# A GpSimd clear of 1024 columns behind each group of four gathers or scatters, in a graph network on one core

## The reference

```python
edge_index = jnp.stack([src, dst])
x = _layernorm(x + _L0_gnn_ref(x, edge_index, ...))                # two GCN layers
x = _layernorm(x + _L1_gnn_ref(x, edge_index, edge_attr_16, ...))  # gated messages, batch norm, layer norm
x = _layernorm(x + _L2_gnn_ref(x, edge_index, edge_attr_16, ...))  # attention with three heads
x = _layernorm(x + _L3_gnn_ref(x, edge_index, batch0, ...))        # six GCN layers, 128-64-32-16-32-64-128
return x

def _gcn_conv(h, W, b, row, col, norm, num_nodes):
    h = h @ W
    msg = h[row] * norm[:, None]
    agg = jax.ops.segment_sum(msg, col, num_segments=num_nodes)
    return agg + b
# gated block: z = concat(x[dst], x[src], edge_attr); msg = sigmoid(z @ Wf.T + bf) * softplus(z @ Ws.T + bs); segment_sum over dst
```

## Time and profile before

| | |
|---|---|
| median of three runs | 11513.55 us (11469.03 to 11515.87) |
| the profiled execution, own time | 11609.91 us |
| its span, first to last instruction | 11608.2 us |
| mean granted TensorE clock | 0.676 of full |
| busy: PE, DVE, ACT, POOL | 57%, 69%, 51%, 64% of the span |
| passes by the span's time | first 0-690, g1 690-1453, g2 1453-2395, gated edges 2395-3562, gated nodes 3562-4751, two attention passes 4751-5701 and 5701-6969, g3 6969-7683, g4 7683-8303, g5 8303-9053, g6 9053-9694, g7 9694-10335, g8 10335-11608 |

### The profile page before, as it was taken

How to read it: one execution, slowest core, us unless ns; L and a number is a source line. 1 busy time by engine, 2 the same in 40 slices (tenths; PEclk the granted TensorE clock), 3 DMA queues, 4 the chain that set the end, 5 groups by cost and what they waited for, 6 DMA issues and landing times. The chain is left out here.

```text
span 11608.2 us, 141508 instructions
## 1 busy us (share of the span) xinstructions
PE 6579.4 (57%) x32436; PEld 5426.1 (47%) x32436; DVE 8028.9 (69%) x33105; ACT 5915.6 (51%) x13869; POOL 7392.5 (64%) x6801
## 2 busy tenths in 40 slices
PE   6036666656664666677656665754455565643343
PEld 3035556645554666677646665642233343422222
DVE  7347799956667999899888884445466666764444
ACT  0024467757667999898667772321133232322222
POOL 7734478867776888666467764556545555556666
PEclk8568888878886555688778885555577555655555
DMA  4977678832224777444345553433344333322221
GB/s 137 302 241 237 235 268 290 289 114 71 71 70 139 236 234 236 144 141 140 107 139 176 176 172 107 136 102 83 85 128 132 89 98 88 120 85 55 56 58 54
DMA packets 1019495, 1694.44 MB, mean 146 GB/s; under 512 B 304877, under 2 KB 535080, under 8 KB 1018594
## 3 DMA queue, kind: packets, MB, share of 16 engines
q1 hardware_dynamic: 782752, 1361.06, 35.0%
q0 software_dynamic: 175936, 218.82, 8.4%
q10 hardware_dynamic: 59970, 105.49, 2.7%
HBM read 988.03 MB, written 707.78 MB: 146 GB/s over the span
## 5 line engine op out<-in xcount | busy, mean ns | idle before, releaser
L1340 POOL DMA_INDIRECT g_got<-scaled,row_src x2352 | 2230.9, 949 | 1651.4 <-issue 679.7
L298 PE MATMUL g_a_p_z<-sb_L_gnn_W,g_a_u_t 128*128 128x128 f32 (+3 forms) x2574 | 653.1, 398 | 1046.4 <-ACT g_a_u_t L1185 375.4
L902 DVE SCALAR_TENSOR_TENSOR g_sums<-g_got,first,g_sums 128x128 f32<-128x128 f32 (+3 forms) x3136 | 869.1, 277 | 395.0 <-issue 111.4
L298 PEld LDWEIGHTS g_a_p_z<-sb_L_gnn_W,g_a_u_t 128*128 128x128 f32 (+1 forms) x2574 | 483.6, 266 | 1219.5 <-issue 562.4
L906 DVE SCALAR_TENSOR_TENSOR g_sums<-g_sums,cont,g_got 128x128 f32<-128x128 f32 (+3 forms) x3128 | 884.7, 283 | 121.6 <-DVE g_sums L902 91.9
L1185 ACT COPY g_a_u_t<-g_a_p_t 128x512 f32<-128x512 f32 (+3 forms) x495 | 225.3, 455 | 1350.4 <-remote 735.5
L298 PE MATMUL g_bb_p_z<-sb_L_gnn_W,g_bb_u_t 128*128 128x128 f32 (+2 forms) x4302 | 836.2, 362 | 121.8 <-DVE g_bb_z L1077 78.6
L298 PEld LDWEIGHTS g_bb_p_z<-sb_L_gnn_W,g_bb_u_t 128*128 128x128 f32 x4302 | 755.8, 262 | 170.9 <-issue 141.7
L1185 ACT COPY g_bb_u_t<-g_bb_p_t 128x1024 f32<-128x1024 f32 (+2 forms) x294 | 233.8, 795 | 1143.2 <-PE g_bb_p_t L289 591.1
L1340 POOL DMA_INDIRECT g_got<-xs,idx_src x392 | 370.8, 946 | 481.4 <-DVE g_a_own L1021 271.3
L1252 POOL DMA_INDIRECT out<-g_a_o,idx_out x396 | 395.3, 998 | 351.6 <-ACT g_a_o L350 222.3
(11 more groups left out here) (495 smaller groups left out, 23743.0 us busy)
## 6 DMA issues: line engine op xcount, KB each, us to landing
raw<-gb_u SPq DMA_DIRECT2D x98, 768.0 KB
xs<-f_o ACTq DMA_DIRECT2D x97, 516.0 KB
f_x<-in_x ACTq DMA_DIRECT2D x97, 512.0 KB
g_bb_own<-in_x SPq DMA_DIRECT2D x97, 512.0 KB
wide<-g_bb_o SPq DMA_DIRECT2D x97, 512.0 KB
g_bb_own<-wide SPq DMA_DIRECT2D x97, 512.0 KB
g_bb_res<-in_x SPq DMA_DIRECT2D x97, 512.0 KB
x<-g_bb_o SPq DMA_DIRECT2D x97, 512.0 KB
```

Of the source, the lines that this page charges most:

```text
L298: last = nc.tensor.matmul(dst_psum[0:p, q * g * width:(q * g + n) * width], turned_tile[0:n * k, q * P:q * P + p], weight[0:n * k, 0:n * w ...
L902: nc.vector.scalar_tensor_tensor(out=self.firsts, in0=new, scalar=first[:, col], in1=self.firsts, op0=ALU.mult, op1=ALU.add).then_inc(run_ ...
L1340: pool.indirect_dma_start(got[b.s4][:, c * row:(c + 1) * row], None, table, bass.IndirectOffsetOnAxis(ap=index[:, b.n * CH + c:b.n * CH + ...
```

## The change

A tile `idle` of 128 partitions by 1024 columns is added to the graph passes and to the gated edge pass. GpSimd clears it behind each block's four gathers in g1 and g3 to g8, behind each block's four scatters in g8, and in the gated edge pass twice a block, behind the four gathers of source rows and behind the four of destination rows. Before each clear it waits for the semaphore increment of the clear before. Nobody reads the tile. g2 is left as it is, as are the passes that are not of these two kinds. That is 98 clears in each of g1 and g3 to g7, 197 in g8 and 196 in the gated edge pass, 981 in all. No other engine's instructions change.

```diff
+REST = 1024
@@ graph_pass
+                idle = sb("idle", [P, REST])
                     def _(pool):
+                        rests = Steps(pool_step, 999)
+
+                        def rest(b):
+
+                            if rests.k:
+                                pool.wait_ge(pool_step, rests.k)
+                            nc.gpsimd.memset(idle[:, :], 0.0).then_inc(pool_step, 1)
+                            rests.count()
+
                         if scatters:
-                            pipeline(pool, [(gather, 0, NBE), (na.scatter, 4, NBA)])
+                            pipeline(pool, [(gather, 0, NBE), (rest, 0, NBE), (na.scatter, 4, NBA), (rest, 4, NBA)])
                             na.scatters_done()
                         elif normal:
...
                         else:
-                            pipeline(pool, [(gather, 0, NBE)])
+                            pipeline(pool, [(gather, 0, NBE), (rest, 0, NBE)])
```

## The result

The changed kernel takes 11157.92 us (median of 4 runs, 11127.33 to 11172.85), the kernel before beside it 11508.53 us (4 runs). The ratio is 0.970, 95% interval 0.968 to 0.972. I had said 11245 us: right in sign, 87 us too high. The profiled execution took 11144.9 us with a span of 11142.8, 465 us less than before. Of these 465 us only 351 are the change: the profiled execution of the kernel before took 11609.91 us, 101 us above its median, and that of the changed kernel 13 us less than its own.

What follows compares the result with a forecast made beforehand. Waits bound the touched passes, as signals are held during GpSimd's descriptor making. Waits -974 and clears +657 give -317; with the gated pass +74 less some 25, about -270: 11610 to 11340, scaled to 11245 us; range 11120 to 11420.

Steps and rivals of the forecast that it cites:

- What bounds the kernel: Touched passes: waits set their length; signals are held while GpSimd makes descriptors; GpSimd's waits in graph passes total 1299 us.
- Cost of a clear: GpSimd's list: a clear takes 0.98 us and adds 0.84 us, 824 us in all.
- The wait for the clear before: Before each clear: taken as 0, at most 1226 us if its signal is held.
- How many of the waits go: Seven graph passes: three quarters of GpSimd's 1299 us of waits go, -974 us; with added clears, -317 us.
- hand-over: Time a held signal needs to pass when GpSimd pauses: 1.25 us after four gathers, 2.4 after 12.
- GpSimd's floor: Each pass's length minus GpSimd's waits plus added clears; the seven graph passes go from 5402 to 4760 us.
- The gated pass: Gated pass: 165 us of clears added, 91 us of waits gone; +74 us, less some 25 for released signals.
- The cover: GpSimd's waits hide the clears; if the waits stay, the clears come on top.
- A: Touched passes: the pause cures everything, every pass at its floor, -568 us, total 10950 us; chance 0.13.
- B: End of the clear: the pause is too short, holds last longer, kernel slower at 11860 us; chance 0.25.
- C: Waits absorb the clears and no more: 650 us go against 657 added, some 11530 us; chance 0.14.
- The rule on ports: g1 and gated pass: a clear could block a two-port VectorE copy; at most 192 us, left out of the sum.

Runs made afterwards that it cites:

- e4: Changed kernel with each of the 981 clears replaced by GpSimd waiting until its four indirect DMAs have landed; 12013.6 us, ratio 1.046 to the kernel before.
- e6: Changed kernel with a clear of 256 columns behind each indirect DMA instead of 1024 behind each four; ratio 0.972 to the kernel before.
- e1: Changed kernel with its 981 clears 16 columns wide instead of 1024; ratio 1.000 to the kernel before.
- e5: Changed kernel without the 196 clears of the gated pass, graph passes as changed; 11085 us, ratio 0.965 to the kernel before.
- e9: Changed kernel with a clear of 128 columns behind each indirect DMA instead of 1024 behind each four; 11428 us, ratio 0.985 to the kernel before.
- e2: Changed kernel with its clears 512 columns wide instead of 1024; ratio 0.984 to the kernel before.
- e7: Changed kernel with one clear of 2048 columns behind each eight indirect DMAs instead of 1024 behind each four; ratio 0.980 to the kernel before.
- e11: On e5, g1 with 256 columns behind each gather, g4 with 512 columns, g8 with 768; 11123 us, ratio 0.959 to the kernel before.
- e10: Graph passes alone, one clear of 4096 columns behind each sixteen indirect DMAs instead of 1024 behind four; 11580 us, ratio 0.998 to the kernel before.

## Why the prediction was right, and where its sizes were off

**What bounds the kernel.** Right: what held the engines was GpSimd's stream of indirect DMAs. Spreading that stream, with nothing else changed, removes the remote waits of g3 to g8 (e4) or of g8 and the gated pass (e6), and adding instructions without time (e1) does not.

**Cost of a clear.** 0.98 us forecast, 0.97 measured; 0.16 us to the next indirect DMA, as forecast; 0.84 us on the list. In g5 GpSimd's busy time grew by 95 us and its 98 shorter gaps gave 14 back, 81 against 82.

**The wait for the clear before.** Taken as 0, measured 0.4 us in all 981.

**How many of the waits go.** This step was mis-sized, by less than the two profiles say. I took three quarters of 1299 us, 974. Between the two profiles 1130 went, and the graph passes became 497 us shorter against a forecast of 317. But the profile before is of an execution 101 us above the median. The kernel with clears of 16 columns (e1, ratio 1.000) has a profile of 11507.6 us, 1 us from that median. Its seven graph passes add up to 5300 us, and its GpSimd waits 1198 us for buffers and scatter rows. Against it the changed kernel's passes are 407 us shorter and some 1030 us of the waits are gone, 86%. So the graph passes brought 90 us more than forecast, and the gated pass cost 14 more; with what the other stretches and the executions differ by, that makes the 87 us by which I was too high. Of the 90 us, 55 are waits; the rest I cannot assign.

Behind it stands a wrong reason: I set the pause of 1.14 us against a hand-over of 1.25 us and called it slightly too short, as if the hand-over were a fixed time. It grows with the run. e6 has pauses of 0.5 us and does nearly as well, so what four leave behind is not a threshold to be met. That the time came out near is in part luck: three quarters was a guess between all and none.

g6 and g7 end at GpSimd's floor (582 and 584 us against a forecast floor of 581 each), g4 at 592 under its floor of 602, g8 at 1183 under 1216. The stretches of the earlier trace rows had made g4's and g8's floors 10 and 20 us too long, and g1's 25 us too short.

**The gated pass.** +49 forecast, +55 measured between the two profiles (+63 against e1's), and e5 takes it away. The floor was the right account: GpSimd waited there for 91 us of remote releases and 20 us of TensorE, these 111 us went, and the clears added 165, which makes +54. The cover was smaller than the cost from the start, as the prediction's own 91 against 165 said; the edit could have been left out there.

**The rivals.** A (everything at the floor) was nearest for g4 and g6 to g8, but g1, g3 and g5 stay 142, 16 and 14 us over the floors forecast (g1 117 us, if its floor is made from the 788 us of the later measure). Only in g1 is that a lot: its 184 us of remote waits were 316. e6's finer spacing takes 38 us more there with 169 us of remote waits, so these do not account for it. B's mechanism was wrong: e6 has no pause over 0.5 us and gains all the same. But it had something real in it: at 0.2 us of added time per indirect DMA the signals pass, at 0.08 to 0.1 (e9, e2) mostly not, and what clears cost is then only partly earned. C: the profile shows no such balance; 1130 us went for 657 added, or 1030 against e1's profile. C's own sum was slightly off: 11610 + 57 = 11667, times 0.9917, is 11570 and not 11530.

**The rule on ports.** It shows, but small, and the prediction's line that VectorE's own durations should not move failed here. VectorE's 128x1024 operations in the gated pass took 1224 ns before and 1215 after (`cg_size`, 96 and 98 of them), and the 98 short copies of that pass (`edge_part`) 164 and 166 ns. The 98 short casts of g1 (`row_src`) went from a mean of 216 ns to 311 and from a longest of 411 to 1426. The longest one, with GpSimd beside it:

```profile
714.92 1.42 DVE L1388 CAST row_src<-g_got 128x4 uint32<-128x4 f32 x1
...
715.35 0.97 POOL L1342 MEMSET g_idle<- 128x1024 f32 x1
...
716.48 0.95 POOL L1351 DMA_INDIRECT g_got<-xs,idx_src  x1 [0.17 <-DVE row_src L1388]
```

The cast ends with the clear, at 716.3, and 12 of the 98 end within 0.1 us of a clear's end. With clears of 2048 columns the mean is 525 ns and the longest 2342; in e4, where GpSimd stands still until the rows have landed, none is over 172. The Trainium skill, page "SBUF — State Buffer", section "Who interferes with whom", would let a clear block a two-port VectorE copy for its length; for these casts the trace agrees. The cost in g1 is at most 98 x 0.095 = 9 us, where I had bounded it at 96, and at most 98 x 0.31 = 30 us with 2048 columns, which can be a part of the 53 us that e7 loses there. It does not explain the held signals: with clears of 16 columns the casts last 220 ns on average and signals are held as before, with 1024 the casts are longer and the held signals fewer.

**What stays open.** That the remote waits follow from GpSimd's pace is shown. What the backlog is, isn't, and it is a picture that fits only in part. Two figures speak for a fixed work per indirect DMA: 1.25 us after 4 and 2.45 after 12, and half the rows change nothing. Three speak against so simple a rule. After runs of 8 in g3 the median is 1.04 us (16 cases), where 0.65 + 8 x 0.15 would be 1.85. Of the 2782 us of remote waits in the seven graph passes of the kernel before, 990 ended while GpSimd went on issuing, with no pause over 0.5 us (201 of 218 us in g4, 386 of 1003 in g8). And g6, at 1.46 us in each case, has 17, 118 or 251 us of remote waits in the profiles of e5, the changed kernel and e11. For g6 to g8 one edge near 1.44 us would do, if g8 is counted by its own interval (28 to 136 us of remote waits at 1.44, none at 1.47; g6 246 to 268 us at 1.43 and 1.44), but g1 and g5 still have 184 and 190 us in the changed kernel. Other layers' nodes run beside g6 and g7 and not beside g8; whether their own signals add to the load was not tried. Why a signal waits out the whole backlog instead of its turn (10 us in e10) is not known either.

## What to carry to other kernels

Where engines that are not busy come free together, shortly after GpSimd's run of indirect DMAs ends, look at how densely these are issued, not at the engine that is late. Time added to the stream can pay, but only in a stretch where GpSimd waits for buffers: compare these waits with the time that you would add, and leave the edit out where they are smaller (111 us against 165 in the gated pass). Then choose the spacing by stretch, at least one pause for each block, and measure on both sides of it, for the edge is sharp (g6: 582 to 599 us at 1.46 us an indirect DMA, 626 at 1.43). And compare profiles of executions that lie at the kernel's median, or the difference of two executions is taken for that of two kernels (here 101 of 465 us).

## What the runs showed of the hardware

- A signal can wait for several microseconds, in g8 up to 15.8 us from the end of its source to the start of the copy, while GpSimd issues indirect DMAs each 1.25 us. Where it passes in a pause, it passes about 0.65 + 0.15 x n us after the last of n (an estimate from the medians at 4 in g1 and 12 in g5; the 1.04 us after 8 in g3 do not fit it).
- In g8 the copies that wait for such a signal start a median of 10.8 us after its source ended; at 1.49 us an indirect DMA none starts more than 0.04 us after it.
- The work behind an indirect DMA goes on after its record ends: behind the fourth, the data had landed only after 3.08 us in the rows of e4. The Trainium skill, page "Perfetto Trace Analysis", section "DMA Instruction — SWDGE (GPSIMD)", says that the record ends when the last descriptor is written, not when the data has moved; the trace agrees.
- An indirect DMA of 64 rows takes 0.90 us, one of 128 rows 0.95; a scatter of 128 rows takes 1.00.
- A clear on GpSimd can stretch a VectorE cast of 128x4 from 0.16 us (median) to 1.42, until the clear ends, and leaves 128x1024 operations as they are (1224 and 1215 ns).
- A clear of 128 partitions took 0.13 us for 16 columns, 0.54 for 512, 0.97 for 1024, 1.83 for 2048 and 3.54 for 4096.
